# Two register loads per expert, moved ahead of the walk over the experts

## The reference

```python
x = hidden_states.reshape(T, H)                      # 1024 x 512
logits = jnp.einsum('th,eh->te', x, router_w)        # 8 experts
probs = jax.nn.softmax(logits.astype(jnp.float32), axis=-1)
top_w, top_idx = jax.lax.top_k(probs, TOP_K)         # TOP_K = 2
top_w = top_w / jnp.sum(top_w, axis=-1, keepdims=True)
g = jnp.einsum('th,eih->eti', x, wg)                 # INTER = 1024
u = jnp.einsum('th,eih->eti', x, wu)
mid = jax.nn.silu(g) * u
expert_out = jnp.einsum('eti,ehi->eth', mid, wd)
out = jnp.einsum('eth,te->th', expert_out, combine)
```

## Time and profile before

| | |
|---|---|
| Median of 3 runs | 1886.89 us (1886.12 to 1889.93) |
| The profiled execution's own time | 1886.4 us |
| Its span, first to last instruction | 1884.7 us |
| Mean granted TensorE clock | 0.934 |
| TensorE busy over the span | 1602.9 us (85%) |
| TensorE busy from 1495 to 1885 us, the walk over the experts | 352.48 of 390 us |
| Instructions of TensorE: matmuls, weight loads | 16191, 16191 |

### The profile page before, as it was taken

One profiled execution on the slowest core, in us unless ns is written; L12 is line 12 of the kernel. 1 busy time (PEld: TensorE's weight loads), 2 busy tenths in 40 slices (PEclk: granted clock), 3 DMA queues, 4 the chain that ended last, 5 costly groups with the idle time before them and its releaser, 6 DMA issues. The chain is left out here.

```text
span 1884.7 us, 43587 instructions
## 1 busy us (share of the span) xinstructions
PE 1602.9 (85%) x16191; PEld 1134.3 (60%) x16191; DVE 1285.4 (68%) x2885; ACT 992.8 (53%) x2210; POOL 682.7 (36%) x795
## 2 busy tenths in 40 slices
PE   6958899999976788659999999769996299989996
PEld 3525566666654566547777777525553278778775
DVE  7858888888854677548888888567776754444441
ACT  5646777777743344336666666433332465555541
POOL 4556676676621111011111111125553123323332
PEclk9979999999996899779999999889998599999998
DMA  5121011111102000021111111431000665565512
GB/s 198 43 72 35 26 44 35 43 38 38 34 24 108 1 2 2 1 67 34 34 34 34 34 34 34 161 115 30 13 13 12 221 197 152 156 182 158 137 30 69
DMA packets 50105, 126.95 MB, mean 67 GB/s; under 512 B 6913, under 2 KB 19553, under 8 KB 49889
## 3 DMA queue, kind: packets, MB, share of 16 engines
q1 hardware_dynamic: 44914, 112.64, 18.5%
q0 software_dynamic: 5008, 11.80, 3.2%
HBM read 110.83 MB, written 15.68 MB: 67 GB/s over the span
## 5 line engine op out<-in xcount | busy, mean ns | idle before, releaser
L106 PE MATMUL e_pGU<-XT,WB 128*128 128x128 f16 x1344 | 232.7, 222 | 18.7 <-issue 8.8
L107 PE MATMUL e_pGU<-XT,WB 128*128 128x128 f16 x1344 | 232.5, 222 | 0.6 <-issue 0.6
L108 PE MATMUL e_pGU<-XT,WB 128*128 128x128 f16 x1344 | 232.5, 222 | 0.0
L2640 DVE SCALAR_TENSOR_TENSOR WB<-w5in,WB 128x1024 f16<-128x1024 f32 x96 | 115.5, 1223 | 85.9 <-ACT WB L2782 85.9
L106 PEld LDWEIGHTS e_pGU<-XT,WB 128*128 128x128 f16 x1344 | 133.8, 100 | 23.9 <-issue 22.4
L107 PEld LDWEIGHTS e_pGU<-XT,WB 128*128 128x128 f16 x1344 | 133.8, 100 | 1.5
L108 PEld LDWEIGHTS e_pGU<-XT,WB 128*128 128x128 f16 x1344 | 133.8, 100 | 0.8 <-issue 0.8
L106 PE MATMUL dpK<-dLT,W 128*128 128x256 f16 x384 | 106.0, 276 | 18.7 <-POOL dLT L1741 18.7
L2623 POOL TENSOR_TENSOR XT<-e_mf,XT 128x256 f16<-128x256 f32 x84 | 56.2, 669 | 173.4 <-ACT XT L2796 173.4
L1752 POOL TENSOR_TENSOR XT<-dzo,XT 128x128 f32 (+1 forms) x32 | 13.7, 427 | 283.9 <-ACT XT L1897 283.9
L734 POOL TENSOR_TENSOR crn<-css,mhalf 128x8 f32<-128x8 f32 x64 | 106.4, 1663 | 5.3
(11 more groups left out here) (556 smaller groups left out, 5746.5 us busy)
## 6 DMA issues: line engine op xcount, KB each, us to landing
w5in<-in_WE SPq DMA_DIRECT2D x96, 512.0 KB, 5.1
cx<-in_ctx SPq DMA_DIRECT2D x32, 384.0 KB, 3.3
dx<-in_ctxT SPq DMA_DIRECT2D x32, 384.0 KB
w5in<-in_W SPq DMA_DIRECT2D x14, 512.0 KB, 8.5
wpiece<-in_W SPq DMA_DIRECT2D x12, 512.0 KB, 9.8
w3in<-in_W SPq DMA_DIRECT2D x11, 512.0 KB, 4.7
cv<-vlat SPq DMA_DIRECT2D x32, 96.0 KB
X<-in_x SPq DMA_DIRECT2D x8, 256.0 KB, 8.6
```

Of the source, the lines that this page charges most:

```text
L106: pe.matmul(out, lh, rh, start=first, stop=False, skip_group_check=shared)
L107: pe.matmul(out, lh, rl, start=False, stop=False, skip_group_check=shared)
L108: return pe.matmul(out, ll, rh, start=False, stop=last, skip_group_check=shared)
L2640: dve.scalar_tensor_tensor(WB[w][:, 1, a], ring[n][:, :], WS, WB[w][:, 0, a], ALU.mult, ALU.subtract)\
```

## The change

All eight pairs of numbers are read in one go where `walk_experts` is called, and kept in registers. `expert` then takes its pair from that list. Nothing else differs.

```diff
         def walk_experts(eng, tile, between=None):
 
 
+            known = [(number(eng, e, SLOTS), number(eng, e + E1, MOST)) for e in range(E1)]
+
             def expert(e, w, nxt):
-                here, ahead = number(eng, e, SLOTS), number(eng, e + E1, MOST)
+                here, ahead = known[e]
                 for s in range(2):
```

## The result

The changed kernel takes 1891.93 us (median of 17 runs, 1888.8 to 1895.14), the one before in the same comparisons 1886.83 (17 runs). The ratio is 1.0027, with a 95% interval of 1.0017 to 1.0037: 3 to 7 us slower. Forecast were 1891 and 4.8 us slower.

A forecast was written before the change was run, and what follows sets the result against it. TensorE was taken to set the pace, with reads on its path at seven boundaries. 9.1 us spent at the start less 4.3 back at the boundaries made 4.8 us slower: 1891 us, range 1884.8 to 1895.7.

The forecast's parts named there:

- Reads on TensorE's path at all seven boundaries: Between experts, each pair of reads delays TensorE's first matmul by 1.3 us; removing seven pairs saves 9.1 us at most.
- the second rival: At the expert boundaries nothing comes back, as something hidden behind the reads holds the first matmul: +9.1, 1895.5 us; chance 0.08.
- 14 reads in front of the first tile: Before the walk's first matmul, 14 TensorE reads at 0.65 us add 9.1 us; bounds 6.6 and 9.8.
- the third rival: Ahead of the first tile, reads take only 0.47 us each and expert 1's clock stays up: -4.2, 1882 us; chance 0.07.
- The other engines' reads are hidden under TensorE's: Before the first tile, ScalarE, VectorE and GpSimd spend 7.8 to 8.8 us on 14 reads, covered by TensorE's 9.1.
- The second block comes late where the landing is near the end of its block: After jumps between experts, TensorE runs out of fetched instructions until the next block, 3.35 to 3.7 us behind the jump's end.
- the first rival: After every jump the next instruction block comes in time, so 9.1 - 9.1 = 0, clock perhaps -0.9: 1886 us; chance 0.29.
- Expert 4: Jump ends on a block's last instruction; first matmul 3.65 us later, eighth at 4.4 instead of 3.35: costs 1.1 us.
- The other experts: Boundaries into experts 1, 2, 5 and 6 gain 1.3 us each, expert 7 gains 0.7, expert 3 costs 0.5.
- The clock: Start -1.1 to +0.6 us, possible 1.75 saved into expert 1, possible drop at expert 3: taken as cancelling.

The follow-up runs named there:

- the kernel before with other landings: Kernel before, reads at every expert, plus never executed filler (90 and 98 transposes) meant to leave 25 instructions of block behind every landing: 1.0068 (1.0048 to 1.0089).
- the changed kernel with room behind each landing: Changed kernel plus 101 never executed transposes in TensorE's code for each expert's fourth tile: 0.9989 (0.9977 to 1.0001) against the kernel before.
- the run with hidden reads: TensorE's sixteen reads moved ahead of its wait for the tables, other engines reading per expert; against the kernel before: 0.9962 (0.9949 to 0.9975).

## Why the prediction was right, and where its sizes were off

- *Reads on TensorE's path at all seven boundaries, 1.3 us each.* Right: 1.8 us from landing to first matmul became 0.5 at the six boundaries that had code to run, which excludes the second rival (nothing comes back). Not right is that each jump ends when the last matmuls of `pY` end: into experts 1 and 4 it ended 2.1 and 3.2 us behind them (1536.36 and 1677.76 against 1534.3 and 1674.6). That part of the idle time is the jump's own, and the change does not remove it.
- *14 reads in front of the first tile, 0.65 us each, 9.1 us.* Right: 0.65 and 9.1. The lower bound of 0.47 us, on which the third rival (faster) rested, is excluded for this place. The Trainium skill states some 200 ns per register in "Runtime: NRT & Kernel Launch", section "Instruction fetch mechanics". For these reads from SBUF the trace does not agree: it shows 0.30 us for the load alone and 0.65 with its two checks.
- *The other engines' reads are hidden under TensorE's.* Right for this kernel, though their price of 7.8 to 8.8 us for 14 does not follow from the load medians given for it. In the changed kernel they stand 0.53 (ScalarE), 0.55 (GpSimd) and 0.64 us (VectorE) apart, 7.5 to 9.0 us for 14. The run with theirs alone shows what is lost without the cover: a wait of 6.4 us at the third group.
- *The second block comes late where the landing is near the end of its block.* This was the step that made the forecast "slower" and not "the same". Shown: filler that is never run removes the gaps, adds them, and puts them where a count of the instructions says. That excludes the first rival (the second block comes in time everywhere).
- *Expert 4.* It was forecast at +1.1; its idle times went from 4.94 + 0.61 to 6.75, +1.2. That this fits so well is luck. The first matmul on the second block came 4.3 us behind the landing and not 3.65, and the eighth 5.0 and not 4.4 (3.33 before). But the part of the jump that lies behind the last `pY` was 0.7 us shorter (2.4 instead of 3.15). The eighth matmul:

```profile
1692.16 0.31 PE L107 MATMUL e_pGU<-XT,WB 128*128 128x128 f16 x1
```

- *The other experts.* Expert 3 was forecast at a wait of 1.8 after 25 matmuls and a cost of 0.5; it waited 1.25 after 23, which leaves -0.15. Two other profiles have 2.1 there, so the block's arrival varies by almost a microsecond. Expert 7 was forecast to run dry after 45 matmuls; it did not. The term that was mis-sized is the count of 1,852 instructions an expert. The trace makes it 1,847, by which expert 7 has 110 instructions left instead of 95 and expert 3 has 50, that is, the 23 matmuls seen.
- *The clock.* Taken as cancelling. Into expert 1 the idle time fell only to 3.16, as its jump took 4.6 us instead of 4.0, and the clock fell all the same (0.50 from 1551 to 1553). Behind expert 4 it came back earlier. TensorE in the changed kernel there, columns as in the earlier trace rows:

```profile
1687.10:1691.40 4.30, 0.00 (x0) 0.53 0.93 246
1691.40:1695.00 3.60, 3.56 (x41) 0.61 0.78 223
```

A mean of 0.61 over 3.6 us is 2.8 us at 0.50 and 0.8 at 1.00, where it was 5.7 us at 0.50 before. That is 1.4 us gained behind this boundary, by the clock alone. Of the 6.1 us that the walk gave back in place of 4.3, the idle times are 5.2: experts 3 and 7 cost less than forecast by 0.65 and 0.6 us, expert 1 gave 0.6 less than its 1.3, and experts 2, 5 and 6 gave 1.3 to 1.5 each. The 0.9 us left over are the clock's: the gain behind expert 4, less some tenths lost in the other experts.

The forecast in total was 4.8 and the runs say 5.1 (3 to 7). In the profiled execution the walk itself lost 3.0. The rest of the difference of the two spans lies in front of the walk, in code that is the same, and single executions of the kernel before differ by up to 11 us. So the agreement to 0.3 us is partly luck; what is established is the sign, the two terms at the start and the boundaries, and the mechanism between them.

Open is what sets the time from a landing to the usable second block. In the 19 late blocks behind a landing in the profiles here, the first matmul on the block came 3.1 to 4.3 us behind the landing. The traces say where that varies: the block's transfer on q8 starts 0.7 to 1.7 us behind the landing, and the matmul comes 2.2 to 3.0 us after that start, in most cases 2.4 to 2.7. The forecast's 3.35 and 3.7 us took this spread for a property of the expert; it is not, as expert 3 shows with 3.2 us in the changed kernel and 4.1 in the two profiles whose gap is 2.1. Busy DMA engines do not explain it alone. They are 93% busy while expert 4 waits in the changed kernel (4.3 us), but 33% in expert 3 of the run with TensorE's reads alone, with nearly the same delay (the gap, and the stretch from the landing on):

```profile
1656.61 0.23 PE L108 MATMUL e_pGU<-XT,WB 128*128 128x128 f16 x1 [2.10 <-issue]
...
1652.50:1656.60 4.10, 1.68 (x25) 1.00 0.33 75
```

No run varied the start of the transfer on purpose.

## What to carry to other kernels

Moving instructions to one place saves nothing if that place is on the critical path too: look for a stretch in which that engine is idle and the numbers are there already (here the last 8 of 15 us ahead of the tables; the reads need 10.5, and another engine's work covered the rest), and check that the engines which get the same move have the same cover. After its jumps, TensorE's instruction queue here had one block and got the next 3.1 to 4.3 us later, so code that was slow to start may have been hiding a fetch; with the delay gone, the position of the landing in its block counts, and never executed instructions can be used to place it. When counting positions, calibrate the count against at least two gaps of the trace, not one.

## What the hardware did that I had not expected

- The position of unchanged code costs up to 13 us or saves 7 in 1890: the kernel before with other landings is at 1.0068, the changed kernel with room behind each landing at 0.9989 instead of 1.0027.
- With a landing on the last instruction of a block, the first matmul is 3.8 to 4.3 us behind it, though the block's transfer itself takes 1.0 to 1.3 us.
- Moving the reads on ScalarE, VectorE and GpSimd alone, 7.5 to 9.0 us each of queue time, costs more (1.0057) than the same with TensorE's (1.0027).
- The clock fell behind a boundary with 2.6 us of idle time. That is the run with hidden reads, into expert 1; the stretch behind the first matmul has a mean clock of 0.66:

```profile
1535.75 0.22 PE L106 MATMUL e_pGU<-XT,WB 128*128 128x128 f16 x1 [2.57 <-issue]
...
1535.70:1539.20 3.50, 3.45 (x42) 0.66 0.67 167
```

Behind a single idle time of 2.3 us (the run with the other engines' reads, into expert 2) it stayed up. The idle time of a boundary does not settle it. In the kernel before with filler, 2.09 and 0.70 us with 12 matmuls between them (into expert 6) left the clock at 1.00; 1.70 and 0.80 us with 15 between them (into expert 7) brought it down to a mean of 0.54:

```profile
1798.30:1801.00 2.70, 2.67 (x48) 1.00 0.74 96
...
1850.30:1853.00 2.70, 2.63 (x27) 0.54 0.81 103
```
